# Routed experts: the second bias moved from TensorE to VectorE

## The chip, the cores and the metric

The kernel runs on one core of a Trainium2 chip. The metric is device time in microseconds of one launch, everything included. A core has a matrix engine (TensorE, "PE" in the profile, with its weight loads as "PEld"), VectorE ("DVE"), ScalarE ("ACT"), GpSimd ("POOL") and SyncE ("SP"), which only issues DMAs here. Each engine runs its own program in order, and the engines wait for each other through semaphores.

## The reference

The reference embeds 64 images as 229 tokens each (one class token, 196 patches, 32 text positions) of width 128, applies a gated attention with a residual, and then a mixture-of-experts layer on all tokens `t`:

```
hs = gelu(t @ sw1.T + sb1)                      # 2 shared experts, F = 512
shared = sum over n of hs @ sw2.T, + sb2.sum(axis=0)
probs = softmax(t @ gate_w.T + gate_b)          # 8 routed experts
top_v, top_i = top_k(probs, 2)                  # weight of an expert = its probability
hr = gelu(t @ rw1[e].T + rb1[e])                # exact gelu, width 512
oe = hr @ rw2[e].T + rb2[e]                     # rb2: the "second bias", 8 x 128
out = h + shared + sum over the top 2 of cw[e] * oe[e]
```

The change is about `+ rb2[e]` and the multiplication by the weight `cw[e]` behind it.

## The kernel before

The program is unrolled and has four stages. In the first (to about 570 us) a loop over 32 pairs of images computes embedding, attention and routing. In the second (to about 800 us) the shared experts of 19 pairs are computed, while POOL scatters every token's row into a DRAM array sorted by expert (`slots_dram`). The third stage, 808 to 1270 us, is that of the **routed tiles**: 122 tiles (`TILES`) of 256 slots, each tile of one expert that is only known at run time. In the fourth the other 13 pairs go through the shared experts, and for each pair the rows of its two routed experts are read from `y_dram`, the second one added by an accumulating DMA, scaled by ACT, added by DVE and stored.

Matrices are fp32 values split into fp16 high and low parts, so that a product is three matmuls (high x high, low x high, high x low).

In the third stage each engine runs a function `step(t, ...)` for each tile, in this order of work:

- **SP**: `load_tile` fetches 256 rows of tile t into one of 8 buffers. It waits until the tile 8 before was transposed, its row numbers copied, and scaled (`x_tr`, `row_set`, `y_ready`).
- **PE**: `up(t)`, two of four blocks of the first product (L1744 to L1746, 12 matmuls of 256 columns per tile); transposes of tile t+2 (L1734); the other two blocks; then `down(t-2)`, the second product of two tiles before: first the *bias product* (L1759, a 128 x 128 matrix of ones times the expert's row of `b2`, 256 columns, which starts the accumulation in the bank), and 24 matmuls of 128 columns (L1767 to L1769). `down` waits for `hid_ready` and, since there are two banks for its result, for `y_ready` of the tile two before its own. `up` waits for `x_ready` and for the gelu of two tiles before.
- **ACT**: four `gelu` instructions of tile t (L1530, each waits for `up_done`), `columns(t+2)` (L1513, copies transposed columns as fp16), and `out_y(t-2)` (L1521, two instructions): waits for `down_done`, copies the result from the PSUM bank to `y_sb`, scaled per row by the routing weight, and signals `y_ready`.
- **DVE**: `split(t)` (L1657 cast and L1659 subtract make high and low of the gelu's result), `y_rows(t)` (L1648), `columns_low(t+2)` (L1664, low part of the columns, signals `x_ready`).
- **POOL**: `scatter_y(t)` (L1444), two indirect DMAs per tile that write `y_sb` into `y_dram`; it waits for `y_ready`, and `y_sb` has 8 slots.

The bias table `b2` is fp16: the program builds in the prologue, on POOL, the high parts in row 0 and the low parts in row 32 of a zeroed 128 x 1024 array (L390, L449 to L455, in steps 3 to 6 of the first loop), so that ones times this array is the bias on every partition.

Which expert a tile has is held in a table of packed words. An engine that needs it loads a word every four tiles and takes three bits of it by shift and mask into a register, scaled to the unit of the table:

```
self.word = self.eng.value_load(experts_word[0:1, bass.ds(j, 1)], ...)
moved = self.word >> (at - to) if at >= to else self.word * 2 ** (to - at)
self.known[n, unit] = self.eng.snap(moved & ((EXPERTS - 1) * unit), ...)
```

PE and ACT have such registers; DVE has none.

Of the kernel before, what the change touches and what calls it, by code (L numbers as in the profile page):

```python
# [23 lines left out]
FP16 = mybir.dt.float16  # L24
# [6 lines left out]
P = 128  # L31
# [28 lines left out]
B2_LO = 32  # L60
B2_COLS = EXPERTS * HID
B2_STEPS = 5
# [43 lines left out]
def build(nc, xmain, xrest, tokw_main, tokw_rest, txt, tokb, token, pos, emb2, emb3, emb4,  # L106
# [6 lines left out]
    with ExitStack() as keep:  # L113
        def sbuf(name, shape, dt=FP32):
# [14 lines left out]
        b2 = sbuf("b2", [P, B2_COLS], FP16)  # L129
# [6 lines left out]
            nc, keep, bank, acc, w_hi, w_lo, b1, ident, top8, slot_2nd, tag_2nd, region_at, next_at, ones, b2, shared_col, row_bufs, slot_1st,  # L136
            xmain, xrest, tokw_main, tokw_rest, txt, tokb, token, pos, emb2, emb3, emb4, w_rel, uv_w, o_w, gamma, beta, g, res,
            gate_w, gate_b, ffn_w, ffn_b1, shared_b2, routed_b2, x2t_dram, x2r_dram, slots_dram)
        experts = experts_and_combine(
            nc, keep, done, bank, acc, w_hi, w_lo, b1, ident, top8, slot_2nd, tag_2nd, region_at, next_at, ones, b2, shared_col, x_cols,  # L140
            row_bufs, x2t_dram, x2r_dram, slots_dram, y_dram, out)
# [29 lines left out]
def embed_and_attend(nc, keep, bank, acc, w_hi, w_lo, b1, ident, top8, slot_2nd, tag_2nd, region_at, next_at, ones, b2, shared_col,  # L171
                     row_bufs, slot_1st, xmain, xrest, tokw_main, tokw_rest, txt, tokb, token, pos, emb2, emb3, emb4,
                     w_rel, uv_w, o_w, gamma, beta, g, res, gate_w, gate_b, ffn_w, ffn_b1, shared_b2, routed_b2,
                     x2t_dram, x2r_dram, slots_dram):

    with ExitStack() as ctx:
# [68 lines left out]
        b2_space = acc[:, NCH - 32:NCH, :].rearrange("p c d -> p (c d)")  # L245
        b2_in = b2_space[:, 0:2 * B2_COLS].rearrange("p (h c) -> p h c", h=2)
        b2_low = b2_space[:, 2 * B2_COLS:2 * B2_COLS + B2_COLS // 2].bitcast(FP16)

# [43 lines left out]
        b2_zeroed, b2_loaded, b2_up = sem("b2_zeroed"), sem("b2_loaded"), sem("b2_up")  # L292
# [20 lines left out]
        def sync(sp, between):  # L313
# [23 lines left out]
            sp.wait_ge(b2_zeroed, 1)  # L337
            for n, row in enumerate((0, B2_LO)):
                sp.dma_start(b2_in[row:row + 1, n, :], routed_b2[0:1, :]).then_inc(b2_loaded, 16)
# [27 lines left out]
        def gpsimd(pool):  # L367
# [22 lines left out]
            pool.memset(b2_space[:, 0:2 * B2_COLS], 0.0).then_inc(b2_zeroed, 1)  # L390
# [50 lines left out]
            def sum_biases(n):  # L441

                if n > 0:
                    pool.wait_ge(b2_up, n)
                if n == 0:
                    pool.wait_ge(b2_loaded, 64)
                    pool.tensor_tensor(shared_col[:, 0:1], shared_col[:, 0:1], shared_col[:, 1:2], ALU.add).then_inc(b2_up, 1)
# [27 lines left out]
            def step(i, p, j, q):  # L475
# [18 lines left out]
                if isinstance(i, int) and 2 <= i < 2 + B2_STEPS:  # L494
                    sum_biases(i - 2)
# [609 lines left out]
class SharedExperts:  # L1105
# [4 lines left out]
    def __init__(self, nc, keep, tag, first, count, flip, up_bank, down_bank, acc, w_hi, w_lo, b1, out_bias, ident, x_cols, gel, hid, y_cols,  # L1110
# [11 lines left out]
        self.gel_ready, self.hid_hi, self.hid_ready = sem("gel_ready"), sem("hid_hi"), sem("hid_ready")  # L1122
# [43 lines left out]
    def split(self, dve, k, parity, j):  # L1166
# [6 lines left out]
        dve.wait_ge(self.hid_hi, self.NJ * k + j + 1)  # L1173
# [51 lines left out]


def experts_and_combine(nc, keep, done, bank, acc, w_hi, w_lo, b1, ident, top8, slot_2nd, tag_2nd, region_at, next_at, ones, b2, shared_col,
                        x_cols, row_bufs, x2t_dram, x2r_dram, slots_dram, y_dram, out):
    LAG, AHEAD = 2, 2
    ROWS_BUFS, TILE_BUFS, Y_BUFS, Y_TILES = 4, 8, 5, 8  # L1230
    assert TILES <= NCH
# [660 lines left out]
```

## Time and profile before

| | |
|---|---|
| median of 3 runs | 1434.36 us (1431.56 to 1438.34) |
| the profiled execution | 1428.73 us |
| its span, first to last instruction | 1427.0 us |
| mean granted clock of TensorE | 0.971 of full speed |
| busy, share of the span: PE | 1246.4 us, 87% |
| PEld | 917.5 us, 64% |
| DVE | 995.4 us, 70% |
| ACT | 812.2 us, 57% |
| POOL | 860.5 us, 60% |

All rows of the trace are from the one profiled execution. Busy time is the sum of instructions on an engine; matmuls are pipelined and their ends are modelled, so a busy PE is not one at its peak. In a wait, what stands behind the arrow is what ended it: "issue" is time in which nothing that the profile shows was waited for, and "remote" a release that the profile could not put down to an instruction of this core.

### The profile page before, as it was taken

How to read it: one execution, taken by the hardware profiler on the slowest of the kernel's cores; microseconds unless marked ns; L12 is line 12 of the kernel's file. 1: busy time of each engine (PE TensorE's matmuls, PEld its weight loads, DVE VectorE, ACT ScalarE, POOL GpSimd, SP SyncE). 2: the span in 40 equal slices, each digit the busy share in tenths (PEclk: the TensorE clock that was granted, in tenths of full speed). 3: DMA queues.
4: the chain of work that ended last, by engine and by line, in shares of the span. 5: the costliest groups of instructions: out<-in, count | busy, mean ns of one | idle time of the engine just before them, and what ended most of it. 6: DMA issues, size and time to landing. Idle time of an engine off the chain costs nothing.

```text
span 1427.0 us, 32972 instructions
## 1 busy us (share of the span) xinstructions
PE 1246.4 (87%) x9758; PEld 917.5 (64%) x9758; DVE 995.4 (70%) x2605; ACT 812.2 (57%) x1966; POOL 860.5 (60%) x820
## 2 busy tenths in 40 slices
PE   5998899999998998799799488888888888899888
PEld 3777677777777777354345377777777777764444
DVE  5787777787777785797477266556655666678776
ACT  2655555555555554555355266666656666667666
POOL 4346656666655554688778466556665665666553
PEclk9999999999999999999899799999999999999989
DMA  6233333333333322243533222222222222219996
GB/s 169 82 114 109 107 111 110 116 129 114 111 109 110 110 70 81 83 109 105 137 102 90 62 74 68 73 68 71 75 72 66 74 77 68 75 51 168 181 192 133
DMA packets 137276, 143.57 MB, mean 101 GB/s; under 512 B 21628, under 2 KB 116473, under 8 KB 137108
## 3 DMA queue, kind: packets, MB, share of 16 engines
q1 hardware_dynamic: 96084, 93.91, 23.2%
q0 software_dynamic: 36992, 40.97, 12.5%
q10 hardware_dynamic: 4032, 6.57, 1.8%
q8 instruction: 90, 1.47, 0.5%
q14 instruction: 78, 0.64, 0.2%
HBM read 86.37 MB, written 55.96 MB: 100 GB/s over the span
## 4 chain that ended last, share of the span: by engine, by line
PE 30%; issue 28%; POOL 24%; DVE 7%; ACT 4%; DMA 3%; another core or an unknown queue 2%; ACTq 1%; SPq 1%; POOLq 0%; DVEq 0%
POOL slots_dram L436 7%; POOL slots_dram L1433 5%; PE bank L1746 4%; PE bank L1744 4%; PE bank L1745 3%; PE bank L1767 3%; DMA scratch<-y_dram 3%; POOL rstd L467 3%; PE bank L1768 3%; PE bank L1769 2%; ACT gel_all L1530 2%; POOL rstd L473 2%; DVE hid_all L1174 2%; POOL emb L406 2%; POOL w_lo L426 2%
## 5 line engine op out<-in xcount | busy, mean ns | idle before, releaser
L1444 POOL DMA_INDIRECT y_dram<-y_sb,y_row x244 | 285.9, 1172 | 189.6 <-ACT y_sb L1521 85.7
L1530 ACT ACTIVATE gel_all<-bank,b 128x256 f32<-128x256 f32 x488 | 196.2, 491 | 80.5 <-PE bank L1746 40.6
L1657 DVE CAST hid_all<-gel_all 128x1024 f16<-128x1024 f32 x122 | 88.7, 727 | 172.0 <-ACT gel_all L1530 163.5
L1163 ACT ACTIVATE gel_all<-bank,b 128x458 f32<-128x458 f32 x256 | 154.3, 640 | 90.5 <-PE bank L1157 54.6
L1433 POOL DMA_INDIRECT slots_dram<-row_bufs,slot_2nd x128 | 153.3, 1197 | 40.1 <-issue 38.0
L1767 PE MATMUL bank<-w_hi,hid_all 128*128 x976 | 176.0, 221 | 1.3 <-issue 0.5
L1769 PE MATMUL bank<-w_hi,hid_all 128*128 x976 | 172.2, 220 | 1.2 <-issue 0.9
L1768 PE MATMUL bank<-w_lo,hid_all 128*128 x976 | 172.1, 220 | 0.8 <-issue 0.7
L1744 PE MATMUL bank<-xT_r,w_hi 128*128 128x256 f16 x488 | 134.3, 275 | 38.6 <-issue 18.4
L436 POOL DMA_INDIRECT slots_dram<-row_bufs,slot_1st x128 | 131.2, 1025 | 38.5 <-issue 38.2
L1659 DVE TENSOR_TENSOR hid_all<-gel_all,hid_all 128x1024 f16<-128x1024 f32 x122 | 149.5, 1225 | 4.2
L1174 DVE TENSOR_TENSOR hid_all<-gel_all,hid_all 128x916 f16<-128x916 f32 x128 | 142.4, 1112 | 4.4
L1746 PE MATMUL bank<-xT_r,w_lo 128*128 128x256 f16 x488 | 134.0, 275 | 5.2 <-issue 5.1
L1745 PE MATMUL bank<-xT_r,w_hi 128*128 128x256 f16 x488 | 133.9, 274 | 5.1 <-issue 4.5
L1172 DVE CAST hid_all<-gel_all 128x916 f16<-128x916 f32 x128 | 83.7, 654 | 73.8 <-ACT gel_all L1163 61.1
L1521 ACT ACTIVATE y_sb<-bank,rows_r 128x128 f32<-128x128 f32 x244 | 78.5, 387 | 92.8 <-remote 72.6
L918 PE MATMUL bank<-xin,tokw 126*128 126x392 f32 (+1 forms) x320 | 115.6, 509 | 10.0 <-DMA tokw<-in_tokw_rest 10.0
L1026 PE MATMUL bank<-kern,v_sb 117*128 117x229 f32 (+1 forms) x512 | 112.9, 364 | 0.8 <-ACT v_sb L827 0.8
L1453 POOL DMA_DIRECT2D scratch<-y_dram x64 | 78.4, 2032 | 57.6 <-DMA scratch<-y_dram 57.3
L1026 PEld LDWEIGHTS bank<-kern,v_sb 117*128 117x128 f32 (+1 forms) x512 | 95.7, 192 | 20.3 <-issue 9.0
L1155 PE MATMUL bank<-x_cols,w_hi 128*128 128x458 f16 x256 | 94.7, 370 | 11.2 <-ACT gel_all L1163 5.7
L1767 PEld LDWEIGHTS bank<-w_hi,hid_all 128*128 128x128 f16 x976 | 96.1, 98 | 12.9 <-issue 10.3
(183 smaller groups left out, 3134.9 us busy)
## 6 DMA issues: line engine op xcount, KB each, us to landing
xin<-in_xmain SPq DMA_DIRECT2D x32, 771.8 KB
rows_r<-slots_dram SPq DMA_DIRECT2D x122, 130.0 KB
x2r_dram<-row_bufs SPq DMA_DIRECT2D x32, 260.0 KB, 2.7
row_bufs<-x2r_dram SPq DMA_DIRECT2D x32, 260.0 KB
x2t_dram<-x2T SPq DMA_DIRECT2D x32, 229.0 KB, 3.0
x_cols<-x2t_dram ACTq DMA_DIRECT2D x28, 229.0 KB
wstage<-in_ffn_w SPq DMA_DIRECT2D x32, 160.0 KB, 2.3
xin<-in_xrest SPq DMA_DIRECT2D x32, 128.6 KB
```

Source lines behind the costliest of these rows:

```text
L436: pool.indirect_dma_start(out=slots_dram, in_=rows_1st[0:m, buf, c, :], in_offset=None, out_offset=bass.IndirectOffsetOnAxis(ap=slot_1st[0 ...
L1026: last = pe.matmul(av_bank[img][:, e * SEQ:(e + 1) * SEQ], v_sb[0:rows, img, c, e * P:(e + 1) * P], kern[0:rows, img, c, :], start=c == 0, ...
L1174: dve.tensor_tensor(lo, self.gel[:, j % 2], hi, ALU.subtract).then_inc(self.hid_ready, 1)
L1433: pool.indirect_dma_start(out=slots_dram, in_=rows_s[0:m, b, c, :], in_offset=None, out_offset=bass.IndirectOffsetOnAxis(ap=slot_2nd[0:m, ...
L1444: pool.indirect_dma_start(out=y_dram, in_=y_sb[:, s, c, :], in_offset=None, out_offset=bass.IndirectOffsetOnAxis(ap=y_row[:, s, c:c + 1], ...
L1530: act.activation(gel[:, s8 % 2, f, :], up_bank[s8 % 2][half][:, (f % 2) * TILE:(f % 2 + 1) * TILE], ACT.Gelu, bias=of_expert(b1, SHARED * ...
L1744: pe.matmul(dst, hi, xT[:, s8 % 4, 0, :], start=True, stop=False)
L1745: pe.matmul(dst, hi, xT[:, s8 % 4, 1, :], start=False, stop=False)
L1746: last = pe.matmul(dst, lo, xT[:, s8 % 4, 0, :], start=False, stop=True)
L1767: pe.matmul(part, h_hi, w2_hi, start=False, stop=False)
L1768: pe.matmul(part, h_hi, w2_lo, start=False, stop=False)
L1769: last = pe.matmul(part, h_lo, w2_hi, start=False, stop=f == NF - 1 and c == TILE_CH - 1)
```

## The change

The bias is no longer a matmul. `b2` becomes a table in fp32, 128 partitions x 1024, loaded by SP with one DMA ahead of the second stage's row loads. `down` begins with its first ordinary matmul. DVE gets the expert registers and a new function `add_bias(t)`: one instruction reads the result of `down(t)` from the bank, adds the expert's bias row and writes `y_sb`; it signals the new semaphore `biased`. It stands at the head of DVE's step, for the tile three before. ACT's `out_y` now waits for `biased` and scales `y_sb` in place; it too runs for the tile three before, where it was two. `down` waits for `biased` where it waited for `y_ready`. `y_sb` no longer has memory of its own but lies in `scratch`, which POOL clears before the tiles. The work of the last tiles that was ahead of or in the late shared experts moves accordingly.

```diff
-                sp.dma_start(b2_in[row:row + 1, n, :], routed_b2[0:1, :]).then_inc(b2_loaded, 16)
-            pool.memset(b2_space[:, 0:2 * B2_COLS], 0.0).then_inc(b2_zeroed, 1)
...
-                elif n == 1:
-                    pool.tensor_copy(b2[:, :], b2_in[:, 0, :]).then_inc(b2_up, 1)
-                elif n == 2:
-                    pool.tensor_copy(b2_low[:, :], b2_in[:, 1, :]).then_inc(b2_up, 1)
-                elif n == 3:
-                    pool.tensor_tensor(b2_low[:, :], b2_in[:, 1, :], b2_low[:, :], ALU.subtract).then_inc(b2_up, 1)
-                elif n == 4:
-                    pool.tensor_tensor(b2[:, :], b2[:, :], b2_low[:, :], ALU.add).then_inc(b2_up, 1)
...
+        b2 = sb("b2", [P, EXPERTS * HID])
-        y_sb = sb("y_sb", [P, Y_TILES, TILE_CH, HID])
+        y_sb = scratch[:, 0:Y_TILES * TILE_CH * HID].rearrange("p (b c d) -> p b c d", b=Y_TILES, c=TILE_CH)
...
+            sp.wait_ge(done.mid_ready, PAIRS)
+            sp.dma_start(b2[:, :], routed_b2).then_inc(b2_in, 16)
             for i in range(PAIRS):
                 load_rows(i)
...
             def out_y(t, s8):
 
-                act.wait_ge(down_done, t + 1)
-                if reaches(t, Y_TILES):
-                    act.wait_ge(y_out[s8], 2 * TILE_CH * (t - s8))
+                act.wait_ge(biased, t + 1)
                 for c in range(TILE_CH):
-                    last = act.activation(y_sb[:, s8, c, :], down_bank[s8 % 2][:, c * HID:(c + 1) * HID], ACT.Copy,
+                    last = act.activation(y_sb[:, s8, c, :], y_sb[:, s8, c, :], ACT.Copy,
                                           scale=rows[:, s8, c, HID + 1:HID + 2])
                 last.then_inc(y_ready, 1)
...
-                if reaches(t, LAG):
-                    out_y(t - LAG, (s8 - LAG) % 8)
+                if t > LAG:
+                    out_y(t - LAG - 1, (s8 - LAG - 1) % 8)
...
+            act.wait_ge(scratch_up, 1)
             tiles(act, step)
 
-            out_y(TILES - 2, (TILES - 2) % 8)
+            out_y(TILES - 3, (TILES - 3) % 8)
...
-                    if k == 0 and f == 3:
-                        out_y(TILES - 1, (TILES - 1) % 8)
+                    if k == 0 and f in (1, 3):
+                        t = TILES - 2 + f // 2
+                        out_y(t, t % 8)
...
+            def add_bias(t, s8, e):
+
+                dve.wait_ge(down_done, t + 1)
+                if reaches(t, Y_TILES):
+                    dve.wait_ge(y_out[s8], 2 * TILE_CH * (t - s8))
+                dve.tensor_tensor(y_sb[:, s8], down_bank[s8 % 2][:, 0:TILE_CH * HID].rearrange("p (c d) -> p c d", d=HID),
+                                  of_expert(b2, 0, HID, HID, e).rearrange("p (c d) -> p c d", c=1)
+                                  .to_broadcast([P, TILE_CH, HID]), ALU.add).then_inc(biased, 1)
...
             def step(t, s8, four):
+                if s8 % 4 == 0:
+                    e = experts.of(1, HID) if t > 0 else None
+                    experts.load(four)
+                elif t > LAG:
+                    e = experts.of(s8 % 4 - 3, HID)
+                if t > LAG:
+                    add_bias(t - LAG - 1, (s8 - LAG - 1) % 8, e)
                 split(t, s8)
                 y_rows(t, s8)
...
             tiles(dve, step)
+            add_bias(TILES - 3, (TILES - 3) % 8, experts.of(TILES - 3 - LAST_WORD, HID))
...
+                    if k == 0 and j < 2:
+                        add_bias(TILES - 2 + j, (TILES - 2 + j) % 8, experts.of(TILES - 2 + j - LAST_WORD, HID))
                     late.split(dve, k, k % 2, j)
...
             def down(t, s8, n):
-                e, e_b2 = experts.of(n, F), experts.of(n, HID)
+                e = experts.of(n, F)
                 s = s8 % 4
                 pe.wait_ge(hid_ready, t + 1)
                 if reaches(t, 2):
-                    pe.wait_ge(y_ready, t - 1)
+                    pe.wait_ge(biased, t - 1)
...
-                pe.matmul(dst.rearrange("p (c d) -> p c d", d=HID), ones[:, :],
-                          of_expert(b2, 0, HID, HID, e_b2).rearrange("p (c d) -> p c d", c=1).to_broadcast([P, TILE_CH, HID]),
-                          start=True, stop=False)
...
-                        pe.matmul(part, h_hi, w2_hi, start=False, stop=False)
+                        pe.matmul(part, h_hi, w2_hi, start=f == 0 and c == 0, stop=False)
...
-            pe.wait_ge(done.b2_up, B2_STEPS)
```

## Rows read from the trace of the kernel before

**Rows 1.** Windows: two stages, us busy and instructions of each engine, clock, DMA.
```profile
808.00:1270.00 462.00, 404.88 (x4761) 344.79 (x4760) 285.91 (x488) 290.28 (x855) 279.78 (x239) 0.99 0.26 69
1277.00:1427.00 150.00, 130.62 (x661) 67.80 (x659) 112.23 (x143) 101.02 (x237) 78.85 (x65) 0.93 0.87 167
```

**Rows 2.** Waits from 850 to 1250 us: total us, times, longest.
```profile
DVE hid_all L1657 <- ACT gel_all L1530: 141.1, 75, 3.6
POOL y_dram L1444 <- ACT y_sb L1521: 74.6, 33, 3.5
ACT y_sb L1521 <- remote: 67.1, 35, 3.3
...
PEld bank L1744 <- issue: 43.2, 66, 1.3
ACT gel_all L1530 <- PE bank L1746: 32.7, 35, 2.9
ACT gel_all L1530 <- remote: 30.3, 17, 3.0
...
ACT y_sb L1521 <- PE bank L1769: 14.3, 17, 1.7
...
PE bank L1744 <- DVE xT_r L1664: 10.0, 18, 0.9
```

**Rows 3.** Timeline of PE: start, duration, line, operation, [idle before].
```profile
841.92 0.27 PE L1759 MATMUL bank<-b,ones 128*128 x1
842.03 0.22 PE L1767 MATMUL bank<-w_hi,hid_all 128*128 x1
...
844.90 0.27 PE L1759 MATMUL bank<-b,ones 128*128 x1
...
846.29 0.22 PE L1769 MATMUL bank<-w_hi,hid_all 128*128 x1
847.24 0.28 PE L1744 MATMUL bank<-xT_r,w_hi 128*128 128x256 f16 x1 [0.73 <-issue]
...
851.18 0.28 PE L1744 MATMUL bank<-xT_r,w_hi 128*128 128x256 f16 x1 [0.48 <-ACT gel_all L1530]
```

**Rows 4.** Timeline of ACT, the same microseconds.
```profile
846.42 0.48 ACT L1513 ACTIVATE xT_r<-bank 128x256 f16<-128x256 f32 x1
849.74 0.62 ACT L1521 ACTIVATE y_sb<-bank,rows_r 128x128 f32<-128x128 f32 x2 [2.85 <-remote]
850.26 1.57 ACT L1530 ACTIVATE gel_all<-bank,b 128x256 f32<-128x256 f32 x4
```

**Rows 5.** Timeline of DVE, the same microseconds.
```profile
846.83 0.68 DVE L1657 CAST hid_all<-gel_all 128x1024 f16<-128x1024 f32 x1
...
848.75 0.42 DVE L1664 TENSOR_TENSOR xT_r<-bank,xT_r 128x256 f16<-128x256 f32 x1
851.86 0.83 DVE L1657 CAST hid_all<-gel_all 128x1024 f16<-128x1024 f32 x1 [2.69 <-ACT gel_all L1530]
```

**Rows 6.** Groups by line and form: count, busy us, mean ns, idle before.
```profile
L1444 POOL DMA_INDIRECT y_dram<-y_sb,y_row x244 | 285.9, 1172 | 189.6 <-ACT y_sb L1521 85.7 <-issue 66.3 <-DVE y_row L1648 37.7
...
L1521 ACT ACTIVATE y_sb<-bank,rows_r 128x128 f32<-128x128 f32 x244 | 78.5, 387 | 92.8 <-remote 72.6 <-PE bank L1769 20.2
...
L1664 DVE TENSOR_TENSOR xT_r<-bank,xT_r 128x256 f16<-128x256 f32 x122 | 50.6, 415 | 16.8 <-ACT xT_r L1513 16.8
...
L1759 PE MATMUL bank<-b,ones 128*128 x122 | 33.8, 277 | 1.0 <-DVE hid_all L1659 0.8 <-issue 0.3
```

**Rows 7.** Groups by line on POOL, 0 to 200 us.
```profile
L455 POOL TENSOR_TENSOR b<-b,acc 128x1024 f16<-128x1024 f16 x1 | 2.1, 2131 | 0.0
...
L390 POOL MEMSET acc<- 128x2048 f32 x1 | 1.8, 1797 | 0.0
```

**Rows 8.** Groups by line, two operations of the later stages.
```profile
L1560 ACT ACTIVATE scratch<-scratch,weight_1st 128x128 f32<-128x128 f32 x128 | 40.1, 389 | 15.5 <-DMA scratch<-y_dram 15.5
...
L1223 DVE TENSOR_TENSOR acc<-acc,bank 128x512 f32<-128x512 f32 x31 | 21.1, 680 | 0.9 <-PE bank L1215 0.9
```

More of the change, by code:

```diff
@@ L59 @@
 WORDS = -(-TILES // 4)
-B2_LO = 32
-B2_COLS = EXPERTS * HID
-B2_STEPS = 5
 EARLY_PAIRS = 19
@@ L336, in sync @@
             load_w(1, 1)
-            sp.wait_ge(b2_zeroed, 1)
-            for n, row in enumerate((0, B2_LO)):
-                sp.dma_start(b2_in[row:row + 1, n, :], routed_b2[0:1, :]).then_inc(b2_loaded, 16)
             for s in range(SHARED):
@@ L439, in scatter_rows, with sum_biases @@
                     ).then_inc(scattered[buf], 16)
[L441 to L447, printed above, removed]
-                elif n == 1:
-                    pool.tensor_copy(b2[:, :], b2_in[:, 0, :]).then_inc(b2_up, 1)
-                elif n == 2:
-                    pool.tensor_copy(b2_low[:, :], b2_in[:, 1, :]).then_inc(b2_up, 1)
-                elif n == 3:
-                    pool.tensor_tensor(b2_low[:, :], b2_in[:, 1, :], b2_low[:, :], ALU.subtract).then_inc(b2_up, 1)
-                elif n == 4:
-                    pool.tensor_tensor(b2[:, :], b2[:, :], b2_low[:, :], ALU.add).then_inc(b2_up, 1)
+            def sum_biases():
+                pool.wait_ge(b2_loaded, 16 * SHARED)
+                pool.tensor_tensor(shared_col[:, 0:1], shared_col[:, 0:1], shared_col[:, 1:2], ALU.add).then_inc(b2_up, 1)
             def keep_top(b):
@@ L493, in step @@
                     sum_text(j + 2)
-                if isinstance(i, int) and 2 <= i < 2 + B2_STEPS:
-                    sum_biases(i - 2)
+                if i == 2:
+                    sum_biases()
             gather_text(0)
@@ L1121, in __init__ @@
         self.up_done, self.down_done = sem("up_done"), sem("down_done")
-        self.gel_ready, self.hid_hi, self.hid_ready = sem("gel_ready"), sem("hid_hi"), sem("hid_ready")
+        self.gel_ready, self.hid_ready = sem("gel_ready"), sem("hid_ready")
+        self.hid_hi = after.hid_hi if after else sem("hid_hi")
         self.y_copied, self.turned, self.acc_done = sem("y_copied"), sem("turned"), sem("acc_done")
@@ L1172, in split @@
         dve.tensor_copy(hi, self.gel[:, j % 2]).then_inc(self.hid_hi, 1)
-        dve.wait_ge(self.hid_hi, self.NJ * k + j + 1)
+        dve.wait_ge(self.hid_hi, self.NJ * (k + (self.after.count if self.after else 0)) + j + 1)
         dve.tensor_tensor(lo, self.gel[:, j % 2], hi, ALU.subtract).then_inc(self.hid_ready, 1)
@@ L1224, in accumulate, with experts_and_combine @@
                           ALU.add).then_inc(self.acc_done, 1)
-def experts_and_combine(nc, keep, done, bank, acc, w_hi, w_lo, b1, ident, top8, slot_2nd, tag_2nd, region_at, next_at, ones, b2, shared_col,
-                        x_cols, row_bufs, x2t_dram, x2r_dram, slots_dram, y_dram, out):
+def experts_and_combine(nc, keep, done, bank, acc, w_hi, w_lo, b1, ident, top8, slot_2nd, tag_2nd, region_at, next_at, ones, shared_col,
+                        x_cols, row_bufs, routed_b2, x2t_dram, x2r_dram, slots_dram, y_dram, out):
     LAG, AHEAD = 2, 2
+    LAST_WORD = (TILES - 1) // 4 * 4
     ROWS_BUFS, TILE_BUFS, Y_BUFS, Y_TILES = 4, 8, 5, 8
@@ L1659, in split @@
                 dve.tensor_tensor(hid[:, s, 1], gel[:, s8 % 2], hid[:, s, 0], ALU.subtract).then_inc(hid_ready, 1)
+            def add_bias(t, s8, e):
[5 more added lines that the diff above has]
+                                  .to_broadcast([P, TILE_CH, HID]), ALU.add).then_inc(biased, 1)
+            experts = Experts(dve)
             def columns_low(t, s8):
@@ L1676, in vector @@
                 columns_low(t, t)
+            dve.wait_ge(tables_up, 3)
+            dve.wait_ge(b2_in, 16)
+            dve.wait_ge(scratch_up, 1)
             tiles(dve, step)
+            add_bias(TILES - 3, (TILES - 3) % 8, experts.of(TILES - 3 - LAST_WORD, HID))
             def add_y(i):
@@ L1689, in vector @@
                 for j in range(NJ):
-                    if k == 1 and j == 0:
-                        dve.wait_ge(down_done, TILES)
+                    if k == 0 and j < 2:
+                        add_bias(TILES - 2 + j, (TILES - 2 + j) % 8, experts.of(TILES - 2 + j - LAST_WORD, HID))
                     late.split(dve, k, k % 2, j)
@@ L1811, in tensor @@
                 late.up(pe, 0, 0, f)
-            pe.wait_ge(y_ready, TILES)
+            pe.wait_ge(biased, TILES)
             for k in range(1, LATE_PAIRS):
```

21 lines of the change are left out of this document (9 added, 12 removed).

## The prediction

> **What bounds the kernel now.** I read the windows first, because the change touches one stage of four. In the two rows of [rows 1] the reader is to see that the routed-tile stage (808 to 1270 us, all 122 tiles) takes 462 us, 3.79 us a tile, in which PE is busy 405, ACT 290, DVE 286 and POOL 280, with the DMA engines at 0.26 and the granted clock at 0.99 (the upper level, 2.4 GHz). No engine fills the stage. The window behind it has DMA at 0.87; the last result rows must have been scattered before it starts, so what the tile stage gains or loses reaches the end nearly one to one.
>
> Next the waits over 106 of the tiles [rows 2]. DVE's first split instruction waits for a gelu in 75 of 106 tiles (141.1 us). ACT's copy-out `out_y` waits 35 times for "remote", 67.1 us, and 17 times for the last down product, 14.3 us; its gelu waits for the up product 35 times and for "remote" 17 times. PE's up product waits for DVE's `columns_low` only 18 times. So the stage is a ring: signal of PE, gelu on ACT, split and `columns_low` on DVE, up product on PE; and PE's signals are often what is late.
>
> The timelines show one turn of this ring. PE, fed, goes from one tile's bias product at 841.92 to the next tile's at 844.90, 2.98 us [rows 3]. The last matmul of the down product behind it starts at 846.29 and ends at 846.51, and the next up product starts at 847.24. ACT had nothing to do after 846.90, yet `out_y` starts only at 849.74, after 2.85 us idle for "remote" [rows 4], 3.2 us behind that down product's modelled end. The gelu behind it in the queue starts at 850.26, 0.52 us later, and DVE's next split at 851.86 [rows 5]. I read this as: the signal of down(8) and that of up(11) come out together at 849.7, and ACT first copies out, then starts the gelu on which the ring turns. I can't see why the signals come late; the page says that ends of matmuls are modelled.
>
> **Removed.** (1) The bias product: 122 matmuls L1759 of 277 ns [rows 6], but pipelined: the next matmul starts 0.11 us behind it (841.92 to 842.03 in [rows 3]), so the most it can give is 122 x 0.11 = 13.4 us, where PE never waits. A fed tile takes 2.98 us and the mean 3.79, so at most a part of tiles are fed; I take a quarter, -3 us (0 to -13). The registers that pick its expert go too; the weight load of L1744 waits 43.2 us for "issue" [rows 2], and their share of it I don't count. (2) Building the fp16 pair in the prologue: a 1.8 us memset and four POOL operations of at most 2.1 us [rows 7] near the start, each in a pair of the attention loop in which POOL has idle time; -1 us (0 to -4, were all but the memset's cover missing). In exchange SP loads 512 KB just ahead of the row loads in the shared-expert stage: +0.5 us (0 to 1).
>
> **Moved.** (3) ACT's `out_y` now stands one step later and waits for DVE. ACT's order is then gelu(t), `columns`(t+2), `out_y`(t-3); what it waits for was produced a step ago. ACT no longer blocks on a late down signal with a gelu behind it. Where the gelu's own input is signalled at the same moment, the ring gets 0.52 us back per turn. The 35 "remote" waits in 106 tiles are 40 in 122, and 40 x 0.52 = 21 us. The 17 short waits on L1769 (0.8 us mean) I leave out, since there the up product was still running; with them it would be 60 x 0.52 = 31 us. None of it is regained if the gelu has to wait as long anyway. I take -21 (0 to -31). The scale itself now reads SBUF in place: its nearest row is L1560, also in place, 389 ns, against L1521's 387 [rows 8, 6]; I cost it at nothing. The Trainium skill, VectorE: DVE Perf Modes, section "The TRN2 errata", speaks against this part: a ScalarE instruction with an SBUF source has a fixed term of 224 cycles, one with a PSUM source 172. By an estimate from that page the 244 copies would take 43 ns more each, 10.6 us of ACT's time in all; the trace does not agree (the two durations above differ by 2 ns), and the sum goes by the trace.
>
> (4) The scatter of tile t-3 follows `out_y`, so POOL starts it up to a step later than now. POOL is busy 280 of 462 us and waits for `y_sb` 33 times; there are 8 slots, so nothing stands behind it until a slot comes round. Two per tile of 1172 ns [rows 6] with a 0.3 us gap is 2.9 us a tile: POOL is the engine that would be the next bound, under a fed tile's 2.98. The load of a tile's rows waits for `y_ready` of 8 tiles before, now one step later; eight tiles of buffers stand against a lookahead of two, so I cost it at nothing; if that cover failed, a step (3.8 us) once. At the end of the stage the last two copies sit behind gelus of the late shared experts: +1 us (0 to 2).
>
> **Added.** (5) On DVE one add a tile, 128 x 256, PSUM plus SBUF. Its nearest row is L1664, the same shape and kinds of operands, 415 ns; upper bound L1223 with 512 columns, 680 ns [rows 6, 8]; lower 265 ns, what the second 256 columns of L1223 cost (680 less 415). It makes DVE's work 286 + 51 = 337 of 462 us. Where is it paid? It stands between `columns_low`(t+1) and split(t). Where DVE waits for a gelu (75 of 106) the add lies in that wait: the down signal that it needs is older than the up signal that gelu needs, and gelu takes 1.57 us more [rows 4]. In the other 31 of 106, 36 of 122 tiles, the split starts right behind `columns_low`, and the split and the next `columns_low` move by 0.42: at most 36 x 0.42 = 15 us. [rows 5] shows such a split (846.83), with `columns_low` behind it at 848.75 to 849.17; the next up product starts at 851.18 (last row of [rows 3]), waiting for ACT. There are 2 us of slack, and the add costs nothing in that pair. I take a quarter: +4 us (0 to +15). If it were on the ring in every tile: +51 us. PE's down(t) now waits for the add of t-2 and no longer for the ACT copy; the add comes right behind `columns_low`(t+2)'s place, before up(t+2) is through: nothing. The expert registers on DVE (a shift and a mask a tile, a load every fourth) have no row of their own; the nearest is PE's weight load of L1744, which has more such work ahead and waits for "issue" 66 times, 43.2 us [rows 2], 0.65 us each. In the same 36 tiles that is 0 to +23 us; since most of it can run while DVE waits or works, I take +1.
>
> **Sum.** -3 - 1 + 0.5 - 21 + 1 + 4 + 1 = -18.5 us. The profiled execution took 1428.73 us (span 1427.0 and 1.7 around it), 5.6 below the median of the three runs, 1434.36. On the profiled execution this gives 1410; on the median, 1415.9. I say 1416.
>
> **Rivals.**
> *Late signals stay, nothing gained.* The signals are late for a cause that is tied to work that stays, and gelu waits in `out_y`'s stead: ACT's 17 remote waits at the gelu and 2.85 us idle are for that. Then terms 3 and 1 are 0 and 5 is small: 1434 + 2, 1430 to 1440.
> *Slower: the add is on the ring.* DVE becomes the engine that sets when up starts. For it: DVE's chain gelu to `columns_low` is 2.5 us a tile, 2.95 with the add, level with a fed PE and POOL; and the 18 waits of PE for `columns_low`. Against: 1.4 us of DVE idle a tile (141.1 us in 106 tiles is 1.33). Price: 0.42 a tile; in half the tiles +26, in all +51 us, less at most 3 for the product: 1457 to 1482. It decides once over 50 tiles pay (50 x 0.42 = 21, all of term 3).
> *Large gain: the late signals go.* If it is the block at `out_y`, or the broadcast product at the head of down, that makes the signals late, tiles go to the fed pitch: 122 x (3.79 - 3.0) = 96 us less, 1338; half of it, 1386. For it: all long idle time of ACT is of this one kind. Against: gelu has it too, where no `out_y` is waited for.
>
> **How the numbers follow.** Forecast (1402 to 1427) 0.43; nothing gained 0.22; slower by the add 0.23; large gain 0.12. A measurement of this kernel tells about 0.5% (7 us) from no change. Faster 0.55, same 0.22, slower 0.23. The range leaves out the far half of the large gain and of the slower case: 1380 to 1458.
>
> **What would show it.** Right: `out_y` on ACT has nearly no wait for "remote"; the split's wait for gelu stays the largest one but shrinks by about the add; the stage takes some 443 us. The add reads 0.41 to 0.43 us. Wrong: gelu's waits on PE or remote grow by the 67 us that `out_y` loses (nothing gained); PE's first up matmul waits for `columns_low` in most tiles (slower); or the mean tile is under 3.4 us (large gain).

## The result, and the profile after

The changed kernel took 1454.78 us (median of 4 runs, 1441.97 to 1455.72) against 1432.96 for the kernel before in the same series, a ratio of 1.0122 with a 95% interval of 1.0089 to 1.0156. The forecast was 1416 us, 1.3% faster; the time went the other way, and lies just inside the upper end of the range (1458). But this is only half of the result: the kernel before took 1429 to 1434 us in the first two series of runs and 1313 to 1316 in most later ones, and there the same change makes the kernel 2% *faster* (ratios 0.9787, 0.9742 to 0.9832, and 0.9801, 0.9761 to 0.9841). Most of what follows is about what lies between the two.

In the first pair of traces the tile stage is where the time went. The view of one line gives the instructions' shortest, median and longest time and the first and last start; here the gelu of the routed tiles after the change (before, the same line starts at 809.2 and 1263.9, as a row further down shows):

```profile
L1512 ACT ACTIVATE gel_all<-bank,b x488: 465/475/527, 801.8 to 1288.7; 128x256 f32<-128x256 f32 x163
```

The tiles start 7.4 us earlier and take 486.9 us where they took 454.7, +32.2; what follows the last gelu takes 165.2 us (163.1 before). That is the 26.9 us between the spans, 1427.0 and 1453.9. The waits after, for the same stretch as [rows 2]:

```profile
POOL y_dram L1428 <- ACT scratch L1503: 143.8, 46, 4.9
ACT gel_all L1512 <- remote: 100.6, 28, 5.1
DVE hid_all L1641 <- ACT gel_all L1512: 92.6, 40, 3.9
...
PE bank L1750 <- DVE xT_r L1659: 26.1, 25, 1.4
DVE scratch L1650 <- remote: 23.7, 18, 3.0
...
ACT scratch L1503 <- DVE scratch L1650: 4.5, 26, 0.2
```

The wait of `out_y` for "remote", 67.1 us before, is gone (4.5 us for the add instead), as the forecast wanted. It has moved, and grown: gelu waits 100.6 us for "remote" where it waited 30.3, the add another 23.7. POOL's wait for `out_y` grew from 74.6 to 143.8 us. The groups of the new and the changed instruction, and of the scatter:

```profile
L1428 POOL DMA_INDIRECT y_dram<-scratch,y_row x241 | 251.5, 1044 | 253.2 <-ACT scratch L1503 187.1 <-issue 66.1
...
L1503 ACT ACTIVATE scratch<-scratch,rows_r 128x128 f32<-128x128 f32 x242 | 85.0, 409 | 10.7 <-DVE scratch L1650 10.7
L1650 DVE TENSOR_TENSOR scratch<-bank,b 128x256 f32<-128x256 f32 x121 | 50.1, 414 | 30.2 <-remote 26.7 <-PE bank L1772 3.5
```

The add takes 414 ns, as estimated (415). The scale in place takes 409 ns, not the 387 of [rows 6]: 22 ns more. The Trainium skill, VectorE: DVE Perf Modes, "The TRN2 errata", has this direction: its fixed term is longer with an SBUF source than with a PSUM source, by 43 ns in my estimate from its cycles. The trace agrees in sign and shows half the size. 244 x 22 ns are 5.4 us of ACT's time in the whole stage, not the cause.

**Where the held signal comes out.** One long wait after the change, on three engines. PE's last matmul of an up product:

```profile
1017.95 0.27 PE L1752 MATMUL bank<-xT_r,w_lo 128*128 128x256 f16 x1
```

ACT, whose gelu needs that product:

```profile
1016.60 0.72 ACT L1503 ACTIVATE scratch<-scratch,rows_r 128x128 f32<-128x128 f32 x2
1021.42 1.57 ACT L1512 ACTIVATE gel_all<-bank,b 128x256 f32<-128x256 f32 x4 [4.10 <-remote]
...
1023.12 0.72 ACT L1503 ACTIVATE scratch<-scratch,rows_r 128x128 f32<-128x128 f32 x2
...
1029.78 0.47 ACT L1512 ACTIVATE gel_all<-bank,b 128x256 f32<-128x256 f32 x1 [2.09 <-issue]
```

and POOL:

```profile
1015.48 1.15 POOL L1428 DMA_INDIRECT y_dram<-scratch,y_row  x1 [1.81 <-ACT scratch L1503]
1016.93 1.11 POOL L1428 DMA_INDIRECT y_dram<-scratch,y_row  x1 [0.30 <-issue]
1018.35 0.97 POOL L1428 DMA_INDIRECT y_dram<-scratch,y_row  x1 [0.31 <-issue]
1019.62 0.97 POOL L1428 DMA_INDIRECT y_dram<-scratch,y_row  x1 [0.30 <-issue]
1024.69 1.13 POOL L1428 DMA_INDIRECT y_dram<-scratch,y_row  x1 [4.09 <-ACT scratch L1503]
1026.13 1.05 POOL L1428 DMA_INDIRECT y_dram<-scratch,y_row  x1 [0.30 <-issue]
1027.48 0.97 POOL L1428 DMA_INDIRECT y_dram<-scratch,y_row  x1 [0.30 <-issue]
1028.76 0.97 POOL L1428 DMA_INDIRECT y_dram<-scratch,y_row  x1 [0.30 <-issue]
```

The up product's matmuls end at 1018.2; gelu starts at 1021.42, 4.10 us idle, 0.8 us after POOL's group of four indirect DMAs is done (1020.59). The next group ends at 1029.73, and the gelu that had waited 2.09 us starts at 1029.78. The kernel before did the same, and I had not laid the two timelines beside each other when I wrote the prediction:

```profile
843.75 0.97 POOL L1444 DMA_INDIRECT y_dram<-y_sb,y_row  x1 [2.05 <-ACT y_sb L1521]
845.03 1.05 POOL L1444 DMA_INDIRECT y_dram<-y_sb,y_row  x1 [0.30 <-issue]
846.38 1.25 POOL L1444 DMA_INDIRECT y_dram<-y_sb,y_row  x1 [0.30 <-issue]
847.94 1.67 POOL L1444 DMA_INDIRECT y_dram<-y_sb,y_row  x1 [0.30 <-issue]
851.20 0.97 POOL L1444 DMA_INDIRECT y_dram<-y_sb,y_row  x1 [1.60 <-ACT y_sb L1521]
```

The group ends at 849.61, `out_y` starts at 849.74 [rows 4]. I read this as POOL being part of the ring in this series: signal, copy-out, scatter, end of the scatter, next signal. Before, POOL began 1.46 us behind the signal (849.74 to 851.20), since `out_y` ran first. After the change `out_y` stands behind four gelus and a column copy, and POOL begins 3.27 us behind it (1021.42 to 1024.69). Over the whole stage two tiles take 7.45 us before (454.7 / 61) and 7.98 after (486.9 / 61).

Two things qualify this reading. First, a few long waits are not all of them. From 850 to 1250 us ACT has 45 waits for "remote" of 1 us or more before and 28 after. 32 and 24 of them end within 1.1 us behind the end of a group of POOL's indirect DMAs, stretches that cover 14% and 15% of the time; 12 and 3 end while a group still runs. So there is a clear tie to the groups, but a signal does not always wait for the end of one: the add below starts 0.6 us before the group's end at 1020.59.

```profile
1019.95 0.42 DVE L1650 TENSOR_TENSOR scratch<-bank,b 128x256 f32<-128x256 f32 x1 [1.08 <-remote]
```

Second, signals are not all that is late. In the same wait PE's own matmuls, which wait for nothing that the profile shows, come 0.7 us apart:

```profile
1019.68 0.22 PE L1771 MATMUL bank<-w_lo,hid_all 128*128 x1 [0.47 <-issue]
...
1020.41 0.22 PE L1770 MATMUL bank<-w_hi,hid_all 128*128 x1 [0.46 <-issue]
...
1021.14 0.23 PE L1772 MATMUL bank<-w_hi,hid_all 128*128 x1 [0.46 <-issue]
```

From 850 to 1100 us PE's weight loads wait for "issue" 52.3 us before and 62.4 after. Where nothing is late (the free series below) this is 13.0 us in the kernel before and 0.4 in the changed one, and with POOL's indirect DMAs replaced by plain ones (e2 and e1) 13.8 and 0.9. So it may be that PE's instructions themselves run late, and their signals with them; the ends of matmuls are modelled, and the runs don't separate the two. "Held" below stands for either.

### The profile page after: what moved, and what is told of

It is laid out like the page before. It is cut to its first block, busy times and chain, and to the rows that moved or that the text cites. A ratio compares the mean times of both kernels' runs of the same rounds, so it can differ in the third digit from the quotient of the medians.

```text
span 1453.9 us, 32936 instructions
## 1 busy us (share of the span) xinstructions
PE 1241.2 (85%) x9636; PEld 910.7 (63%) x9636; DVE 1034.2 (71%) x2727; ACT 825.0 (57%) x1966; POOL 823.8 (57%) x815
## 4 chain that ended last, share of the span: by engine, by line
issue 27%; POOL 27%; PE 21%; ACT 6%; another core or an unknown queue 5%; DVE 5%; DMA 3%; ACTq 1%; SPq 0%; DVEq 0%; POOLq 0%
POOL slots_dram L1417 9%; POOL slots_dram L425 7%; ACT gel_all L1512 3%; PE bank L1752 3%; PE bank L1750 3%; DMA scratch<-y_dram 2%; POOL rstd L445 2%; POOL rstd L451 2%; PE bank L1751 2%; POOL emb L395 2%; POOL w_lo L415 2%; PE bank L1771 2%; PE bank L1772 2%; PE bank L1770 2%
## 5 line engine op out<-in xcount | busy, mean ns | idle before, releaser
L1428 POOL DMA_INDIRECT y_dram<-scratch,y_row x244 | 255.1, 1045 | 256.8 <-ACT scratch L1503 190.1
L1770 PE MATMUL bank<-w_hi,hid_all 128*128 x976 | 176.8, 221 | 13.5 <-issue 13.4
L1772 PE MATMUL bank<-w_hi,hid_all 128*128 x976 | 175.7, 221 | 13.0 <-issue 12.7
L1771 PE MATMUL bank<-w_lo,hid_all 128*128 x976 | 175.8, 221 | 10.9 <-issue 10.8
L1641 DVE CAST hid_all<-gel_all 128x1024 f16<-128x1024 f32 x122 | 85.7, 702 | 139.4 <-ACT gel_all L1512 113.2
L1750 PE MATMUL bank<-xT_r,w_hi 128*128 128x256 f16 x488 | 137.1, 281 | 44.4 <-DVE xT_r L1659 33.4
L1751 PE MATMUL bank<-xT_r,w_hi 128*128 128x256 f16 x488 | 136.7, 280 | 6.0 <-issue 5.9
L1772 PEld LDWEIGHTS bank<-w_hi,hid_all 128*128 128x128 f16 x976 | 96.5, 99 | 18.8 <-issue 18.6
L1771 PEld LDWEIGHTS bank<-w_lo,hid_all 128*128 128x128 f16 x976 | 96.5, 99 | 18.7 <-issue 17.3
L1770 PEld LDWEIGHTS bank<-w_hi,hid_all 128*128 128x128 f16 x976 | 96.6, 99 | 17.0 <-issue 13.0
```

Of the source, the lines that this page charges most:

```text
L1428: pool.indirect_dma_start(out=y_dram, in_=y_sb[:, s, c, :], in_offset=None, out_offset=bass.IndirectOffsetOnAxis(ap=y_row[:, s, c:c + 1], ...
L1750: pe.matmul(dst, hi, xT[:, s8 % 4, 0, :], start=True, stop=False)
L1751: pe.matmul(dst, hi, xT[:, s8 % 4, 1, :], start=False, stop=False)
L1770: pe.matmul(part, h_hi, w2_hi, start=f == 0 and c == 0, stop=False)
L1771: pe.matmul(part, h_hi, w2_lo, start=False, stop=False)
L1772: last = pe.matmul(part, h_lo, w2_hi, start=False, stop=f == NF - 1 and c == TILE_CH - 1)
```

## The experiments

Theories: **A**, PE's end signals are held while POOL runs indirect DMAs, and the later `out_y` makes POOL start later; **B**, the add is on DVE's part of the ring; **C**, without the bias product PE's instructions come late. All comparisons are with the kernel before in the same series, with a 95% interval. "Held" is a series in which the kernel before takes over 1420 us, "free" one in which it takes about 1314.

| run | series | before | this | ratio |
|---|---|---|---|---|
| changed kernel | held | 1433 | 1454.8 | 1.0122 (1.0089 to 1.0156) |
| e1_after_plain | held | 1429 | 1317.3 | 0.9199 (0.9141 to 0.9258) |
| e2_before_plain | held | 1429 | 1354.2 | 0.9458 (0.9405 to 0.9511) |
| e3_before_out_y_later | held | 1429 | 1455.4 | 1.016 (1.010 to 1.022) |
| e4_before_no_product | held | 1429 | 1416.1 | 0.9905 (0.9865 to 0.9946) |
| e9c_idle_add_third | held | 1464 | 1475.7 | 1.0068 (1.0044 to 1.0091) |
| e5_after_out_y_first | free | 1313 | 1544.5 | 1.1764 (1.1737 to 1.179) |
| e6_after_add_twice | free | 1313 | 1293.4 | 0.9843 (0.982 to 0.9866) |
| e7_after_again | free | 1315 | 1287.7 | 0.9787 (0.9742 to 0.9832) |
| e6b_add_twice_again | free | 1315 | 1291.4 | 0.9815 (0.9768 to 0.9862) |
| e8_after_half_scatter | free | 1315 | 1284.2 | 0.9758 (0.971 to 0.9807) |
| e10_before_again (one run, for its trace) | free | 1315 | 1312.1 | none |
| e9_before_idle_add | free | 1315 | 1315.4 | 1.0005 (0.998 to 1.003) |
| e3b_out_y_later_again | free | 1315 | 1319.0 | 1.003 (1.0007 to 1.0054) |
| e4b_no_product_again | free | 1315 | 1286.4 | 0.9777 (0.9739 to 0.9814) |
| e9b_idle_add_again | free | 1316 | 1317.4 | 1.0013 (0.9989 to 1.0038) |
| e8b_half_scatter_again | free | 1316 | 1289.3 | 0.9785 (0.9757 to 0.9813) |
| e7b_after_third | free | 1316 | 1292.0 | 0.9801 (0.9761 to 0.9841) |
| e8c_half_scatter_third | free | 1316 | 1284.8 | 0.9772 (0.9735 to 0.9809) |

### The scatter without POOL (e1, e2)

```diff
-            for t in range(TILES):
-                scatter_y(t)
+            def store_y(t):                      # issued by SP, behind load_tile(t + 8)
+                sp.wait_ge(y_ready, t + 1)
+                for c in range(TILE_CH):
+                    sp.dma_start(y_dram[at + c * P:at + (c + 1) * P, :], y_sb[:, s, c, :]).then_inc(y_out[s], 16)
```

> The changed kernel with POOL's two indirect DMAs per tile replaced by two plain DMAs of the same bytes that SP issues, to rows in tile order (so the routed results land in the wrong rows of y_dram). Theory A (POOL on the ring): in the tile stage PE's end signals are held back while POOL runs a burst of indirect DMAs, and come out at its end. Then without the bursts gelu's waits for remote nearly vanish, a tile takes 3.0 to 3.2 us, and the time falls by 70 to 90 us, to 1360 to 1385. Theory B (the add is on DVE's part of the ring): POOL is a passenger, the time stays within 10 us of the changed kernel's 1454.

> The kernel before with the same replacement of POOL's scatter by plain DMAs issued by SP. Theory A: out_y's wait for remote (67 us) vanishes, the time falls by 60 to 85 us, to 1350 to 1375; and the difference between this and the changed kernel with plain stores is what the change costs or gives with POOL out of the way: by theory A within 8 us of zero, by theory B the changed one is still 20 us or more slower. If POOL is a passenger, this stays at 1433.

Both fell as theory A says, e1 by more than it said (1317 us against 1360 to 1385). One part of A's forecast missed: the two should have been within 8 us of each other, and the changed kernel is 37 us faster. The gelu line of the two, the changed kernel first, then the one of before:

```profile
L1521 ACT ACTIVATE gel_all<-bank,b x488: 466/474/512, 803.0 to 1155.6; 128x256 f32<-128x256 f32 x163
```

```profile
L1539 ACT ACTIVATE gel_all<-bank,b x488: 465/474/511, 812.3 to 1196.4; 128x256 f32<-128x256 f32 x163
```

352.6 and 384.1 us: with POOL out of the way no wait for "remote" is left from 850 to 1100 us, and the change makes the stage 31.5 us shorter, in the same condition in which it makes it 32.2 us longer with the scatter on POOL. The condition had not gone away in these two: their tiles start at 803.0 and 812.3 us, as in the first pair of traces (801.8 and 809.2) and not as in free ones (about 771). Yet the tile stage itself is as long as in free traces, where it takes 352.9 us with the change (e7) and 381.3 without (e10): all that the held condition adds to this stage goes with the indirect DMAs. Theory B falls as the main cause: e1 has the add too, and loses nothing by it. What exactly of the indirect DMAs holds the signals (POOL's instruction, its descriptors, their transfers) the runs don't separate.

### One part alone (e3, e4)

```diff
-                if reaches(t, LAG):
-                    out_y(t - LAG, (s8 - LAG) % 8)
+                if t > LAG:
+                    out_y(t - LAG - 1, (s8 - LAG - 1) % 8)
```

> The kernel before with one thing of the change alone: ACT's out_y one step later (from the bank, with the bias product kept, no work on DVE). Theory A: POOL's burst starts later in the ring, so that the held signals come later: 10 to 25 us slower than before, about 1450. Theory B: no slower than before, 1412 to 1436. Theory C (the missing bias product lets PE's sequencer fall behind): 1430 to 1436.

```diff
-                pe.matmul(dst..., ones[:, :], of_expert(b2, ...)..., start=True, stop=False)
...
-                        pe.matmul(part, h_hi, w2_hi, start=False, stop=False)
+                        pe.matmul(part, h_hi, w2_hi, start=f == 0 and c == 0, stop=False)
```

> The kernel before without the bias product alone (the second bias of the routed experts is left out). Theories A and B: 0 to 13 us faster than before, 1420 to 1433. Theory C: slower, 1440 to 1455, with waits for issue ahead of the down matmuls of over 20 us, as in the changed kernel.

The later `out_y` alone costs 1.6%, all of the change's loss and more. Its waits, for 850 to 1100 us, show the same move: none of `out_y`, and for the gelu and POOL

```profile
POOL y_dram L1444 <- ACT y_sb L1521: 63.9, 18, 4.4
ACT gel_all L1530 <- remote: 52.5, 21, 4.6
```

Part of it may not be the hold: PE also waits 14 times for `out_y`, 10.0 us in these 250, because here the bank is freed a step later; in the changed kernel the add frees it. The free series (e3b, below) shows what this does without a hold: 4 us.

Leaving out the product alone gives 0.95%, 13.6 us by the ratio, 4 us below the range of theories A and B (1420 to 1433), and theory C is out. The gelu lines of the kernel before, e3 and e4 (three kernels, a fence for each):

```profile
L1530 ACT ACTIVATE gel_all<-bank,b x488: 465/478/562, 809.2 to 1263.9; 128x256 f32<-128x256 f32 x163
```

```profile
L1530 ACT ACTIVATE gel_all<-bank,b x488: 464/473/545, 810.3 to 1295.2; 128x256 f32<-128x256 f32 x163
```

```profile
L1530 ACT ACTIVATE gel_all<-bank,b x488: 465/477/564, 808.8 to 1255.3; 128x256 f32<-128x256 f32 x163
```

454.7, 484.9 and 446.5 us: +30.2 and -8.2 in the stage, by one trace of each.

### Free series: the order on ACT, and the add (e5, e6, e7, e9)

```diff
+                if t > LAG:
+                    out_y(t - LAG - 1, (s8 - LAG - 1) % 8)
                 gelu(t, s8, e, 0)
...
                     columns(t + AHEAD, (s8 + AHEAD) % 8)
-                if t > LAG:
-                    out_y(t - LAG - 1, (s8 - LAG - 1) % 8)
```

> The changed kernel with ACT's out_y of tile t-3 ahead of the gelus of step t, where it was behind them. Theory A: POOL's burst starts 1.5 us or more earlier in the ring, 15 to 30 us faster than the changed kernel, 1425 to 1440. Theory B: gelu now also waits for the add, so 10 to 30 us slower than the changed kernel, 1465 to 1485.

```diff
+                dve.tensor_tensor(scratch[...free part...], down_bank[...], of_expert(b2, ...)..., ALU.add)
                 dve.tensor_tensor(y_sb[:, s8], down_bank[...], of_expert(b2, ...)..., ALU.add).then_inc(biased, 1)
```

> The changed kernel with DVE's add done twice per tile, the first time into a free part of scratch (51 us more DVE work). Theory A: the add stands where DVE mostly waits: 0 to 12 us slower than the changed kernel, up to 1466. Theory B: the added 0.42 us is paid in half the tiles or more: 25 to 51 us slower, 1480 to 1505.

The same chip ran the kernel before in 1313 us here, 116 us less than in e1 to e4. The doubled add, which could only cost, came out 1.6% faster than the kernel before, so I ran the changed kernel beside it:

> The changed kernel unaltered, once more. The kernel before took 1429 us in the first series and 1313 in the second, so this ties the two. Where the kernel before takes about 1430, it takes 1446 to 1456 here. Where it takes about 1313, theory A (PE's held signals are what makes the change slower) wants it faster than before, 1285 to 1300; theory B (the add on the ring) wants it no faster than before, 1313 or more.

> The changed kernel with the add done twice, once more, now beside the changed kernel. Theory A: within 12 us of the changed kernel on the same chip. Theory B: 25 to 51 us slower than it.

The changed kernel is 2.1% faster, the second add costs 3.7 us by the medians, within theory A's 12. In the window from 850 to 1100 us of each I count the instructions of DVE, the third number in brackets, first in the changed kernel and then in the kernel before (e10, another chip in the free condition):

> The kernel before unaltered, for its trace in this series. Where it takes about 1313: theory A wants PE's signals on time, so no waits of out_y and gelu for remote and a tile of about 3.0 us (with the bias product PE's own pitch, 2.98). Where it takes about 1430, the waits for remote are as in the first trace, 60 us or more for out_y.

```profile
850.00:1100.00 250.00, 249.93 (x3274) 234.10 (x3272) 228.97 (x431) 209.26 (x604) 196.04 (x172) 1.00 0.35 92
```

```profile
850.00:1100.00 250.00, 245.18 (x3108) 223.30 (x3107) 184.79 (x318) 197.32 (x557) 188.84 (x159) 1.00 0.32 86
```

With 5 and 4 DVE instructions a tile, 431 and 318 of them are 86.2 and 79.5 tiles in 250 us: 2.90 and 3.14 us a tile (about 3.0 was expected of the second), PE busy 100% and 98%. No row for "remote" is among the waits of either. POOL in the changed kernel runs its indirect DMAs without a pause:

```profile
900.06 1.29 POOL L1428 DMA_INDIRECT y_dram<-scratch,y_row  x1 [0.30 <-issue]
901.65 0.97 POOL L1428 DMA_INDIRECT y_dram<-scratch,y_row  x1 [0.30 <-issue]
902.93 1.28 POOL L1428 DMA_INDIRECT y_dram<-scratch,y_row  x1 [0.30 <-issue]
904.52 0.97 POOL L1428 DMA_INDIRECT y_dram<-scratch,y_row  x1 [0.30 <-issue]
905.80 1.28 POOL L1428 DMA_INDIRECT y_dram<-scratch,y_row  x1 [0.30 <-issue]
```

2.87 us a tile. So POOL's indirect DMAs are not enough to make signals late: in the free series they stand back to back, and nothing is late. With e1 and e2 they are needed for it, but something in the condition of the chip has to be there too.

e5 is a miss of both theories' numbers, and by a ring that I had not seen: `out_y`(t-3) ahead of gelu(t) waits for the add, which stands behind the split of t-1 on DVE, which waits for gelu(t-1). ACT and DVE then take turns, 5.0 us a tile, in a free series. Its largest wait for 850 to 1100 us is that of the copy for the add, 131.1 us in 50 tiles. In this design the add needs a step between it and what reads it, and that is what puts the scatter late.

The idle add measures the added DVE work alone, on the kernel before (DVE also waits once, before the tiles, for POOL to have cleared `scratch`):

```diff
                 if t == 0:
                     early.accumulate(dve, EARLY_PAIRS - 1)
+                if t < TILES - 1:
+                    dve.tensor_tensor(scratch[...], top8[:, 0:32, :], top8[:, 32:64, :], ALU.add)   # 413 ns
```

> The kernel before with an idle add of 256 fp32 columns a tile on DVE (both operands and the result in unused SBUF; nothing waits for it), at the place in DVE's order that the bias add has after the change: behind columns_low, ahead of the next split. It measures term 5 by itself. Theory A: 0 to 8 us slower than before. Theory B: 25 to 51 us slower.

> The kernel before with the idle add on DVE, once more, for the condition in which the kernel before takes about 1430. There, with the ring turning through DVE, theory A gives 0 to 8 us slower and theory B 25 to 51. Where the kernel before takes 1313: the same time as before, again.

> The kernel before with the idle add on DVE, a third time, in case the kernel before takes about 1430 here. Then theory A: 0 to 8 us slower; if the add is what the other parts leave unexplained, 10 to 15 us slower. Where the kernel before takes 1313: no difference, as twice before.

Nothing in the two free series; in the third the kernel before took 1464 us, signals were held (the gelu waits for "remote" 42.0 us in 250), and the add cost 0.68%, 10 us: above theory A's 0 to 8, at the lower end of the 10 to 15 that what the other parts leave open would want.

### The parts again in the free condition, and half the scatter (e3b, e4b, e7b, e8)

> The kernel before with out_y one step later alone, once more. It was 1.6% slower than before where that took 1429. Theory A: where the kernel before takes 1313 there are no held signals and it is within 6 us of it. Theory D (the later out_y costs by itself, through the later scatter or the banks): again 15 us or more slower.

> The kernel before without the bias product alone (the routed experts' second bias left out), once more. At 2.98 us a tile PE sets the pace, and 0.11 us a tile is 13 us: 1298 to 1304 where the kernel before takes 1314. If registers and waits of the product count too, up to 0.2 us a tile: 1288 to 1296.

The later `out_y` costs 0.3% where nothing is held (4 us by the medians; 1.6% where signals are held). Leaving out the product gives 2.2%: 28 us, 0.23 us a tile, twice what its matmul's place in the pipeline is worth and a little more than the upper 0.2 of the expectation. By the gelu line the stage takes 381.3 us in e10 (771.0 to 1152.3), 382.4 with the later `out_y` and 354.2 without the product: +1.1 us for the first, where the held traces gave +30.2.

```diff
-            for t in range(TILES):
+            for t in range(0, TILES, 2):          # into an array that nobody reads
                 scatter_y(t)
```

> The changed kernel with POOL's indirect DMAs kept for even tiles only (into an array that nobody reads); SP issues plain DMAs of as many bytes for the odd ones, so the routed results are in the wrong rows. Theory A: POOL's bursts are half as long (2 DMAs, 2.3 us, where they were 4, 5.3 us), most PE signals come on time, and the time is nearer to the one with plain stores only (1317) than to the changed kernel's: 1320 to 1370 where the kernel before takes 1430. If only the number of DMAs counts and not the length of a burst, half way: about 1385.

> The changed kernel with POOL scattering the even tiles only, once more, for the condition in which the kernel before takes about 1430 and PE's signals are held. There theory A gives 1320 to 1370. If the number of DMAs counts and not the length of a burst: about 1385. Where the kernel before takes 1313: 1284 again.

> The changed kernel unaltered, in the series that follows one in which the kernel before took 1464 us. Theory A: as in the first series 10 to 30 us slower than the kernel before if that takes 1430 or more; 25 to 30 us faster if it takes 1313.

> The changed kernel with POOL scattering the even tiles only. If PE's signals are held in this series (the kernel before at 1430 or more), theory A gives 1320 to 1370, since a burst is 2 DMAs; if only the number of indirect DMAs counts, about 1385 or more. If they are not held, 1285 as before.

The half scatter ran in three series and the changed kernel once more, and all fell into free series. Half the scatter takes 1284 to 1289 us, the changed kernel 1288 to 1292. The question that the half scatter was for, whether a burst's length sets the hold, stays open.

## Why the prediction was wrong

**The ring.** I wrote that PE's signals come late and that I couldn't see why, and then costed the move as if their lateness stayed fixed in time. Shown: without POOL's indirect DMAs it is gone (e1, e2). The trace of the kernel before would have told: most of ACT's long waits end just behind a group of POOL's. The time lies in the stated range by luck: its upper part was there for an add on the ring, 1457 us and more, which is not what happened.

**Term 3, `out_y` a step later: -21 us.** This is the step that failed. Alone it measured +1.6%, 23 us, in the held series and +0.3% in the free one. The block at `out_y` did go; but ACT then waited longer at the gelu for a signal that mostly comes out with POOL's end, and POOL's start had moved back by 1.8 us in the turn read above. That the later `out_y` costs, and only where signals are held, is shown; that it costs by way of POOL's later start is read from the timelines, and no run moved POOL's start by itself.

**Term 4, the later scatter: nothing.** The same error from the other side. "Nothing stands behind it until a slot comes round" is true of semaphores, and no semaphore carries the dependence that e1 shows. The rival "late signals stay" had the right place (gelu waits in `out_y`'s stead) and the wrong price, since it took the scatter's time as given.

**Term 1, the product: -3 (0 to -13).** Undersized: -13.6 us held, -28 us free. The bound of 0.11 us a tile left out the registers; 0.23 us a tile in the free series is more than the matmul's slot. The traces point at them: from 850 to 1100 us the waits of the weight loads for "issue" fall from 13.0 us (e10) to 1.1 us (e4b). No run takes the registers out alone.

**Term 5, the add: +4 +1.** Inside its bounds: 0 and +2 us in the free series, 10 us in a held one. The rival that gave 26 to 51 us for it fell; the change came out slower by another mechanism.

**Term 2, the prologue: -0.5.** Undersized in the held condition: the tiles start at 801.8 and 803.0 us in its two traces with the change, at 808.8 to 812.3 in the four of the first two series without it (before, e2, e3, e4): some 7 us earlier. In the one free series that has traces of both, they start at 770.0 without it (e9) and 767.1 and 768.6 with it (e7, e6b), 1 to 3 us; over all free traces the starts with it (767.1 to 772.9) and without (770.0 to 773.7) overlap. POOL has idle time in the pair (6.20 us ahead of L426), but not where the operations stood: they come behind the work that depends on DVE, right ahead of the row scatter of their pair. Before:

```profile
108.12 1.03 POOL L449 CAST b<-acc 128x1024 f16<-128x1024 f32 x1
...
109.52 1.08 POOL L436 DMA_INDIRECT slots_dram<-row_bufs,slot_1st  x1 [0.22 <-issue]
```

After:

```profile
107.15 1.08 POOL L425 DMA_INDIRECT slots_dram<-row_bufs,slot_1st  x1 [0.22 <-issue]
```

The first row scatter is 2.4 us earlier. 1.4 us of it are there before this pair of the loop begins (the same POOL instruction, L426 before and L415 after, starts at 86.07 and 84.66); that could be the memset's 1.8, which was not covered either. How the rest of the 7 us comes about was not followed.

**The sum by parts**, held, in the stage: later `out_y` +30.2, product -8.2, together +22.0; the change measured +32.2. The 10.2 left are about what the idle add cost in another held series (0.68% of 1464, 10.0 us); the two series are not the same one, so this is consistent and not proven. The granted clock from 850 to 1100 us was also lower, 0.95 after the change against 0.97 in e3 and 0.99 before, and nothing here tells its share. Free: product -28, later `out_y` +4, add 0 to +2, prologue -1 to -3 make -23 to -27; measured -27.2 (1287.7 against 1314.9).

**Open:** how the indirect DMAs make PE's signals late, and what puts a chip in the held or the free condition. The chip that showed the held one in e1 to e4 (1429 us) and e9c (1464) ran the kernel before in 1313 in between (e5, e6); the three others of the later series were always free. In the held traces what stands ahead of the tiles is longer too (they start at 809.2 and 832.5, free at 771.0), so it isn't a matter of the tile stage alone.

Of the kernels that leave nothing out the changed one is the fastest in the free condition and the kernel before in the held one. The part that gains in both, dropping the product, needs the bias from somewhere that does not put the scatter later; I tried none that does.

## What to carry to other kernels

When a signal is late and the profile names no cause, lay the timelines of all engines over one long wait, those included that wait for nothing here: if one engine's work ends where most of the waits end, it may be in the ring, and moving its start may move the signal: take that work out in a trial to see. A move that only makes a store later is free by semaphores and may not be free in time. And measure the kernel before again in each series: the sign of this change hangs on the condition of the chip, which only the time and the waits of the kernel before tell here.

## What the runs showed of the hardware

- The same kernel took 1313, 1430 and 1464 us in different series, at a mean granted clock of 0.971 in its trace at 1429 us and 0.977 in that at 1312: the clock is not the difference. In the slower condition a signal of PE reached ACT 3.2 us behind the modelled end of its matmuls (846.51 to 849.74, and 1018.22 to 1021.42), 0.1 and 0.8 us behind the end of POOL's group of indirect DMAs. With these replaced by plain DMAs from SP, the same kernel took 1354 us where it took 1429, and the changed one 1317.
- PE's weight loads waited for "issue" 52.3 us of 250 in the slower condition, 13.0 in the faster one, and 13.8 in the slower one without the indirect DMAs.
- A 128 x 128 fp32 scale on ACT took 409 ns from SBUF to SBUF and 387 from PSUM to SBUF.
- Leaving out a matmul of 256 columns, pipelined at 0.11 us, together with its expert register gave 0.23 us a tile of end-to-end time (e4b) where PE was busy 98% of the time.
